# One copy of the high query rows in the wide cross attentions, and the second group's weights issued behind the first query stack

## The reference

```python
def _attn(x, ctx, Wq, Wk, Wv, Wo, bo, heads):
    q = (x @ Wq).reshape(b, n, heads, -1)
    k = (ctx @ Wk).reshape(b, j, heads, -1)
    v = (ctx @ Wv).reshape(b, j, heads, -1)
    scale = q.shape[-1] ** (-0.5)
    sim = jnp.einsum('bihd,bjhd->bhij', q, k) * scale
    attn = jax.nn.softmax(sim, axis=-1)
    out = jnp.einsum('bhij,bjhd->bihd', attn, v).reshape(b, n, -1)
    return out @ Wo + bo
x = _attn(h, context, q2, k2, v2, o2_w, o2_b, H) + x
```

## Time and profile before

| | |
|---|---|
| median of 3 runs | 4615.15 us (4612.82 to 4621.1) |
| the profiled execution | 4592.06 us, its span 4590.2 us |
| PE busy | 4082.9 us, 89% of the span |
| DVE, ACT, POOL busy | 67%, 45%, 29% |
| layer 2's cross attention | from 2715 us to about 3053 us |
| layer 3's cross attention | from 4128 us to about 4437 us |

### The profile page before, as it was taken

How to read it: one execution, slowest core, us unless ns; L and a number is a source line. 1 busy time by engine, 2 the same in 40 slices (tenths; PEclk the granted TensorE clock), 3 DMA queues, 4 the chain that set the end, 5 groups by cost and what they waited for, 6 DMA issues and landing times.

```text
span 4590.2 us, 56559 instructions
## 1 busy us (share of the span) xinstructions
PE 4082.9 (89%) x20828; PEld 2498.1 (54%) x20828; DVE 3092.3 (67%) x4625; ACT 2079.0 (45%) x3756; POOL 1347.2 (29%) x664
## 2 busy tenths in 40 slices
PE   7999989789998887998999977888999999987889
PEld 5343356634334675555555545666555555546668
DVE  5888855688885666777777854455677677774355
ACT  2555644355565443444444435553344444434541
POOL 1100011100000124655555543421344444441120
PEclk7999989999998998999999988998999999998999
DMA  4223231123223332233222324423322222216420
GB/s 129 40 42 49 44 58 35 43 30 56 41 29 55 57 61 65 64 65 66 61 63 63 65 51 109 97 70 70 69 65 65 66 65 65 58 39 153 95 62 19
DMA packets 158515, 286.64 MB, mean 62 GB/s; under 512 B 36458, under 2 KB 70052, under 8 KB 157216
## 3 DMA queue, kind: packets, MB, share of 16 engines
q1 hardware_dynamic: 158240, 283.03, 29.6%
HBM read 105.01 MB, written 29.64 MB: 29 GB/s over the span
## 4 chain that ended last, share of the span: by engine, by line
PE 61%; DVE 16%; issue 6%; ACT 5%; POOL 5%; SPq 4%; DMA 2%; DVEq 0%; POOLq 0%; ACTq 0%
PE PS L993 26%; PE PS L1173 12%; PE PS L1069 4%; PE PS L1215 4%; PE PS L1065 4%; PE PS L1303 3%; DVE t L1733 3%; PE PS L1225 2%; DVE t L1729 2%; SPq L2179 1%; POOL t L1997 1%; SPq L2162 1%; DVE PS L1818 1%; POOL t L2024 1%; POOL t L2011 1%
## 5 line engine op out<-in xcount | busy, mean ns | idle before, releaser
L993 PE MATMUL PS<-t 128*128 128x512 f32 (+4 forms) x7896 | 1983.8, 382 | 152.6 <-ACT t L1446 30.4
L1446 ACT ACTIVATE t<-PS 128x512 f32<-128x512 f32 (+2 forms) x1600 | 1165.4, 749 | 1107.8 <-PE PS L993 1101.8
L993 PEld LDWEIGHTS PS<-t 128*128 128x128 f32 (+2 forms) x7896 | 1242.5, 186 | 700.5 <-issue 256.7
L1173 PE MATMUL PS<-t 128*32 128x512 f32 (+2 forms) x4352 | 812.3, 612 | 0.2
L1729 DVE TENSOR_REDUCE t<-PS 128x1 fp32r<-128x1024 f32 x512 | 621.4, 1219 | 267.9 <-PE PS L1065 261.0
L1733 DVE TENSOR_REDUCE t<-PS 128x1 f32<-128x512 f32 x1024 | 649.3, 682 | 72.4 <-PE PS L1069 70.8
L2024 POOL TENSOR_TENSOR t<-t 128x1024 f32<-128x1024 f32 x256 | 618.0, 2414 | 125.8 <-ACT t L1446 99.1
L1069 PE MATMUL PS<-t 96*128 96x512 bf16 x1024 | 372.4, 396 | 31.0 <-DVE t L1733 13.2
L1065 PE MATMUL PS<-t 128*128 128x512 f32 x1024 | 336.8, 411 | 46.0 <-DVE t L1729 26.8
L2020 POOL TENSOR_TENSOR t<-t 128x1024 f32<-128x1024 f32 x64 | 156.1, 2439 | 744.4 <-PE PS L1183 468.2
L1961 POOL TENSOR_TENSOR t<-t 128x2048 f32<-128x2048 f32 x24 | 109.5, 4564 | 833.0 <-DMA t<-in_rows 564.6
(11 more groups left out here) (134 smaller groups left out, 3950.0 us busy)
## 6 DMA issues: line engine op xcount, KB each, us to landing
t<-t SPq DMA_DIRECT2D x256, 256.0 KB, 3.9
t<-t SPq DMA_DIRECT2D x512, 128.0 KB, 3.7
t<-scr_n SPq DMA_DIRECT2D x288, 128.0 KB, 6.3
scr_n<-t SPq DMA_DIRECT2D x72, 256.0 KB, 2.2
t<-t SPq DMA_DIRECT2D x256, 64.0 KB, 2.1
t<-in_L_Wg SPq DMA_DIRECT2D x16, 768.0 KB, 4.6
t<-in_L_W SPq DMA_DIRECT2D x36, 256.0 KB, 3.2
t<-in_L_Wo SPq DMA_DIRECT2D x64, 128.0 KB, 2.7
```

The costliest lines, as they stand in the source:

```text
L993: ins = e.matmul(out, l, r, start=i == 0, stop=i == len(terms) - 1, tile_position=tp)
L1173: ins = e.matmul(banks[S.ot][wd * j:wd * j + wd, :], u.v[j][kt], P[0:S.pr, j, :], start=kt == 0, stop=kt == S.nkt - 1, tile_position=(0, w ...
L1446: e.activation(dst, src, ACT.Exp, scale=S.L.scale).then_inc(*expd.inc((S.i, i)))
```

## The change

The stack of a wide cross attention loses its slot 1: `[128, 2, 1, S.qw]`. The second product of `cs` reads slot 0, whose other rows meet zeros in the keys' low table. The four transfers of a pair that wrote both slots by a broadcast write one. The six memsets of each stage go, and with them the wait on `zeroed` ahead of a `cs`. In the plan, `w_load` of group 1 stands behind `qstack` of pair 0.

```diff
-                S.QS = [sbt(c, [128, 2, 2, S.qw], F32R) for _ in range(S.nqs)]
+                S.QS = [sbt(c, [128, 2, 1, S.qw], F32R) for _ in range(S.nqs)]
...
-                              (qs[0:lim[j], j, 1, q0 + 128 * t:q0 + 128 * t + 128],
+                              (qs[0:lim[j], j, 0, q0 + 128 * t:q0 + 128 * t + 128],
...
-                    plan.put(-9, -9, [("w_load", p, 1), ("qstack", S, 0), ("qstack", S, 1), ("w_split", p, 1, 1)]
+                    plan.put(-9, -9, [("qstack", S, 0), ("w_load", p, 1), ("qstack", S, 1), ("w_split", p, 1, 1)]
...
                 kv_ready(w, S, u.pi % 8 // 2)
-                w.wait_ge(zeroed, S.i)
...
-                for q in S.QS:
-                    e.memset(f(q[0:64, 1, 1, :]), 0.0).then_inc(*zeroed.inc(S.i))
                 if S.cross:
                     K = S.kv
-                    for q in S.QS:
-                        e.memset(f(q[64:65, 0, 1, :]), 0.0).then_inc(*zeroed.inc(S.i))
...
                 else:
+                    for q in S.QS:
+                        e.memset(f(q[0:64, 1, 1, :]), 0.0).then_inc(*zeroed.inc(S.i))
...
-                        for dst, at in ((o[x:x + 32, jj, :, :], f(src[r, 0:1, q]).broadcast_to([32, 2, S.qw])),
-                                        (o[x + 32:x + 64, jj, :, :], f(src[r, 1:2, q]).broadcast_to([32, 2, S.qw])),
+                        for dst, at in ((o[x:x + 32, jj, :, :], f(src[r, 0:1, q]).broadcast_to([32, o.shape[2], S.qw])),
+                                        (o[x + 32:x + 64, jj, :, :], f(src[r, 1:2, q]).broadcast_to([32, o.shape[2], S.qw])),
```

## The result

| | before | after |
|---|---|---|
| median of 22 runs each | 4608.95 us (4597.26 to 4621.1) | 4621.02 us (4609.53 to 4629.1) |
| the profiled execution | 4592.06 us | 4626.94 us |

The ratio of the two is 1.0025, with an interval from 1.0017 to 1.0033: about 12 us slower, just over what a measurement of this kernel can tell. The median of before over 22 runs is 6.2 us under that of the first three.

The account below looks back on a forecast made before the run. PE was taken to bound most of the span, with chains of small steps at stage starts. Layer 2's 5.9 us and layer 3's 5.5 us gave 11.4 us on 4615.15 us: 4626.5 us, 0.25% slower, range 4613 to 4635 us.

Parts of the forecast that it names:

- What bounds the kernel: At both cross stages' starts, group 1's weights are on the path; the first stack is needed only after them.
- The price of a stack: On SP's queue, a 1 MB stack of eight transfers takes 5.3 us, against 7.3 us before; issuing sets the pace.
- The landing: From issuing group 1's weight load behind the stack to the start of its split: 3.3 us.
- Layer 2: Start of layer 2's cross stage: group 1 and everything behind it late by 5.9 us.
- Layer 3: Start of layer 3's cross stage: group 1 late by 8.8 us, 0.72 and 2.57 us given back, 5.5 us net.
- The memsets: Six DVE memsets dropped at each start: 0 us, covered by POOL in layer 2 and a wait for ACT in layer 3.
- The clock at the starts: Longer idle ahead of group 1 may keep PE at half clock: 0 added, at most 1.7 us.
- Steady state, 0 us: Over each stage's 16 stacks, each 2.0 us shorter on SP: nobody waits for them, so 0 us.
- The two stages get longer by 5.9 and 5.5 us: Sign to look for: layer 2's and layer 3's cross stages lengthen by these amounts, all else keeps its length.
- the absorbed case: Rival, 0.25: PE's later waits for POOL have slack and absorb layer 3's delay (4621 us) or both layers' (4615 us).
- That the stacks pace the units: Rival, 0.08: SP's queue, freed of 64 us through both stages, sets the pace; 4562 us if all showed.
- The full queue: Rival, 0.07: single copies are held back at SP's queue as before; 4634 us, or 4638 us with the clock.

Follow-up runs that it names:

- the kernel that has it: Against before, only group 1's weights moved behind the first stack, which keeps its two copies of the high rows; ratio 1.0036 (1.0024 to 1.0048).
- The first run of that kernel: Single copies with group 1's weights first, plus a staging tile of their own and an early load in layer 2; ratio to before 0.9938.

## Why the prediction was right

The forecast was 0.25% slower and the runs say 0.25%. In microseconds it was 4626.5 against 4621.02, since the three runs it stood on had a median 6.2 us above that of the 22. The mechanism is the one that was told: group 1's weights are on the path, and a stack ahead of them delays them by its issue. That even the second digit agrees is luck, since the interval is from 0.17% to 0.33% and some steps were off. The steps:

- **What bounds the kernel.** Right. With the order undone the starts are those of before, with one more stack ahead they are later by one more stack, and with an early load group 1 starts 12.0 and 13.2 us sooner in layer 2.
- **The price of a stack.** 4.98 us for 5.3 us. The eight transfers are issued at 0.62 us each. More bytes than in the self attention's stack (1 MB for 0.75 MB) took no more time (4.98 us for 5.21 us), so the bytes don't set this pace. That they did with two copies is seen where the same eight transfers take 7.38 us. The Trainium skill, "SBUF — State Buffer", section "Door 1: The DMA port swizzle", led to an estimate of 4.8 us for the moving of 1 MB. That is near 4.98 us, and the share of 0.91 is near full, so issuing sets the pace by little, as was said.
- **The landing.** 3.25 and 3.00 us for 3.3 us.
- **Layer 2.** 5.7 us for 5.9 us.
- **Layer 3.** Group 1 8.5 us late for 8.8 us; given back by the second transposition 2.0 us for 2.6 us, the DVE wait of 5.58 us and the stack's 0.72 us gone as foreseen. 6.0 us for 5.5 us. Sum of both layers: 11.7 us for 11.4 us. The 0.72 us was counted in full, and only 0.4 us came back by the first transposition.
- **The memsets.** Predicted 0 us, and the runs show no cost that they can tell from none. The reason was too narrow: POOL's cover depends on how fast PE's opening products run, and where they took 5.69 us, 1.46 us stuck out.
- **The clock at the starts.** No cost seen: the row of 40 products (group 1's 24 and the first 16 of the scores) took 9.73 us after 22.82 us of waiting and 10.46 us after 17.25 us.
- **Steady state, 0 us.** This was too little. "Nobody waits for them" missed 1.8 us for which ACT waited for a stack's transfers in layer 3 (L1400), and the clock was thought to cost, not to give back. From the second to the eighth transposition of layer 3 before took 56.5 and 56.3 us (clock 0.92 and 0.93), the two profiles of after 55.6 and 54.0 us (0.94 and 0.97). So at the eighth after is late by 5.1 and 3.1 us, and not by the 6.0 and 5.6 us of the second. In layer 2 the same stretch differs by 2.8 us between the two profiles of before, so nothing can be read there.
- **"The two stages get longer by 5.9 and 5.5 us"** can't be read in a pair of profiles. Over all of them it fits: layer 3's stage, to the end of the span, has a mean of 462.6 us in the two profiles of before and of 468.0 us in the five with single copies and the move in layer 3 (464.1 to 471.1 us). With single copies and the weights first it has 454.2 us in four, which is again more than the starts show.

Of the rivals, the absorbed case falls as it was told. PE's waits for POOL took up nothing in layer 2 (41.7 us for 41.6 us) and 1.8 us in layer 3 (30.4 us for 32.2 us), which the forecast had counted. Some of layer 3's shift is lost further back all the same, by another way (the clock, as above), and the timed 12 us say that most of it stays. That the stacks pace the units falls with the single copies alone, 0.12% faster where a third of the 64 us would have been 0.45%. The full queue falls with 4.98 us, and the kernel that has it costs 0.36%.

## What to carry to other kernels

In a queue that is worked off in order, a load on the path that stands behind transfers nobody needs yet is late by their whole issue time, and the work behind it shifts by nearly all of that. Look for what the first long idle of a stage waits for, and put its load ahead, in a buffer of its own if the shared one holds it back: here that was worth 20 to 23 us against the kernel with single copies and the weights first (0.9938 and 0.9945 against 0.9988), nearly twice what the change lost. Where two profiles of one kernel differ by more than the effect, measure distances within a stage, and leave the size to the timed runs.

## What the runs showed that was not expected

**Two profiles of one program differ by 16 us.** Before has spans of 4590.2 and 4606.2 us at mean clocks of 0.951 and 0.950, after 4625.2 and 4607.1 us. Over the profiles of all kernels the opening 24 products of layer 2's stage took between 5.69 and 8.59 us.

**DVE and POOL hold each other up.** The two subtractions of group 1's split (DVE L1651, 128x256 each) took 2.77 us while POOL's L2011 and L2012 ran, and 0.76 us in after, where POOL was idle. The first run of that kernel has 2.77 us too. The loss of 2.0 us is most of the 2.48 us for which POOL worked meanwhile (2729.48 to 2731.96). It is on the path: the split ends at 2732.25, and PE's wait of 4.23 us ends at 2732.34. The Trainium skill, "SBUF — State Buffer", section "Who interferes with whom", says that a DVE instruction with two inputs in SBUF and a GpSimd instruction that reads SBUF exclude each other for a whole instruction. The rows agree with it. No run here moved the split away from POOL's work, so the cause stays argued.

**A stack's push-back on SP.** Eight issues of SP took 4.98 us with 1 MB and 7.38 us with 1.5 MB, and a load of 256 KB behind them needed 3.25 us and 4.50 us to be seen by its reader.
